# Experts' outputs by accumulating scatters: a two-layer decoder on one core, rows added in memory in place of gathers and sums

## The chip, the cores and the metric

One core of a Trainium2 chip runs the whole program. The metric is the device time of one execution in microseconds (us), the median of several runs. Engines are named as the profile names them: PE (TensorE), DVE (VectorE), ACT (ScalarE), POOL (GpSimd), SP (SyncE, which here only issues transfers).

## The reference, cut to what matters

`x` holds 4 batches of 512 tokens of 512 floats. Six sublayers follow one another, each added to its input:

```python
x = x + attn0(layernorm(x))              # linear attention and softmax attention
x = x + graph(ctx_512, layernorm(x))     # graph mixing
x = x + moe(layernorm(x))                # the experts
x = x + attn1(layernorm(x))              # self attention
x = x + xattn1(layernorm(x), ctx_512)    # causal cross attention
x = x + ffn1(layernorm(x))               # gated network with a Walsh-Hadamard transform
```

The part that the change touches is `moe`, cut to its core (T = 2048 tokens):

```python
scores = softmax(x @ w_cls.T)                       # 64 choices: 32 experts, 32 that give nothing
_, topk_idx = top_k(scores + bias, 8)
w = scores[topk_idx]; w = w / (w.sum(-1) + EPS) * 1.5
routed = topk_idx < 32
w_r, w_z = where(routed, w, 0), where(routed, 0, w)
# up to CAP = 256 tokens of each expert, in the order of their numbers
y = (silu(g) * u) @ w_down                          # g, u = split(rows @ w_gate_up)
out = sum over the 8 choices of w_r * y[expert, place] * (1 + w_z.sum())
```

## The kernel before, in words

The program is a chain of stages with a barrier between them, each a function: linear attention (names with `a_`), `graph_and_router` (`gr_`, L1543), `experts` (`ex_`, L2396), `attention_layers` (`at_`, L195), `network` (`ff_`). All matrices are float32; a product is made of three matmuls of high and low parts (`_hi`, `_lo`), and the parts are split off by ACT (high) and DVE or POOL (low).

**Router.** `graph_and_router` treats a batch of 512 tokens (4 tiles of 128) at a time. In `router` (L2171 to L2272) DVE takes the 64 biased scores of each token, finds the 8 largest and their numbers (`max`, L2198, and `max_index`, L2202), makes one-hot rows `hot` of 32 choices x 64 (L2206), sums them to `mask` (L2209), multiplies `hot` with the scores (L2220) and reduces (L2221) to the 8 weights; PE counts each expert's earlier tokens (`choices`), and from the places DVE makes two things: the table `index`, which says for each of the 32 x 256 slots which token fills it (`write_rows`, L2274), and `slots`, which says for each of a token's 8 choices in which slot its output will lie (`slot_numbers`, L2252 to L2261). `weights` keeps the 8 weights of a token. In between, DVE searches the 153rd largest value of half of the graph's rows (`max` and `match_replace`, L2050, L2056), and ACT and POOL that of the other half by bisection; the two meet at L2101. On POOL, `blocks_hot` (L2345 to L2355) waits for DVE's row numbers, and `rstds` (L2341) for its statistics. The layer normed rows go to `normed` in memory, one row of 512 floats for each token behind a row 0 of zeros, and x to `x_after_graph`.

**Experts.** 32 experts in turn, two buffers (`u`). POOL gathers the expert's 256 rows of `normed` by two indirect transfers (L2645, four experts ahead), PE transposes them (L2505) and makes the products, POOL splits off the low part of `w_down` (`split_d`, L2635, two experts ahead), SP loads 1.5 MB of weights for each (L2455). The output y is copied from PSUM by ACT (tile 0, L2577) and DVE (tile 1, L2610), and SP stores its 512 KB to `out_rows` (L2461). Between two experts DVE makes two steps of the Walsh-Hadamard transform of another layer's weights (`butterfly`, L2622). The engines' programs are straight queues: an instruction that waits holds all behind it on its engine.

**Attention.** For each batch, each token's 8 output rows are gathered from `out_rows` by `slots` (POOL, `gather`, L262 to L272: 32 transfers of 128 rows a batch) and added into x with their weights (DVE, `add_rows`, L274 to L291, 32 times `scalar_tensor_tensor`), and x goes back to memory by `store_sum` (L293) as the residual that `load_residual` reads later. Batch 0 is done in a block of its own, `first_sums` (L297 to L313), before anything else of the attention; batches 1 to 3 are spread over the steps of the attention by `SUMS_AT` and `sums_at` (L355 to L361). A step `g` is one of 4 groups of heads of a batch, three steps ahead of the softmax for the projections. Layer norm is `measure`, `statistics`, `layernorm` (L731 to L750).

```python
SUMS_AT = {1: 0, 6: 1, "mid_end": 2, "end": 3}     # L355: after which pair of a step the adds stand
first_sums: load x of batch 0; 32 gathers; 32 adds, 4 bn_stats; 4 stores of 256 KB
```

## Time and profile before

| | before |
|---|---|
| median of 3 runs | 3035.86 us (3032.19 to 3039.69) |
| span of the profiled execution | 3028.2 us, 7.7 us under that median |
| mean granted clock of TensorE | 0.900 |
| PE busy | 2476.7 us (82%) |
| DVE busy | 1884.0 us (62%) |
| ACT busy | 1239.5 us (41%) |
| POOL busy | 851.9 us (28%) |
| written to memory | 62.92 MB |
| read from memory | 182.30 MB |

The span of the profiled execution runs from its first to its last instruction; its own time as a run is not listed apart from the three. The stages lie at 0 to 655 us (linear attention), 655 to 1140 (graph and router), 1140 to 1482 (experts), 1482 to 1536 (`first_sums`), 1536 to 2493 (the two attentions) and 2493 to 3028 (network). A share of busy time is a mean over stages that have different limits, so each stage has to be read by itself.

### The profile page before, as it was taken

How to read it: one execution, taken by the hardware profiler on the slowest of the kernel's cores; microseconds unless marked ns; L12 is line 12 of the kernel's file. 1: busy time of each engine (PE TensorE's matmuls, PEld its weight loads, DVE VectorE, ACT ScalarE, POOL GpSimd, SP SyncE). 2: the span in 40 equal slices, each digit the busy share in tenths (PEclk: the TensorE clock that was granted, in tenths of full speed). 3: DMA queues.
4: the chain of work that ended last, by engine and by line, in shares of the span. 5: the costliest groups of instructions: out<-in, count | busy, mean ns of one | idle time of the engine just before them, and what ended most of it. 6: DMA issues, size and time to landing. Idle time of an engine off the chain costs nothing. (4 is left out here: it accounts for less than half of the span.)

```text
span 3028.2 us, 35090 instructions
## 1 busy us (share of the span) xinstructions
PE 2476.7 (82%) x12822; PEld 1644.7 (54%) x12822; DVE 1884.0 (62%) x2959; ACT 1239.5 (41%) x1873; POOL 851.9 (28%) x1176
## 2 busy tenths in 40 slices
PE   5898989864443357999448999999999879999999
PEld 4454545321222237998334554545555538888887
DVE  3766575627899985778557777565655444444443
ACT  2444444428656625666103433334333323333332
POOL 2232222215657634555343332001211110000000
PEclk8999999976665678999768999999999979999999
DMA  3213132212222346988585655334433423101000
GB/s 117 65 43 84 43 84 46 70 61 77 77 80 77 108 163 213 308 300 289 158 185 136 159 146 157 88 89 104 109 95 91 115 80 127 42 0 42 1 28 15
DMA packets 186940, 323.55 MB, mean 107 GB/s; under 512 B 20450, under 2 KB 52066, under 8 KB 186788
## 3 DMA queue, kind: packets, MB, share of 16 engines
q1 hardware_dynamic: 168356, 270.44, 30.0%
q0 software_dynamic: 15360, 50.34, 6.3%
q8 instruction: 88, 1.44, 0.2%
q10 hardware_dynamic: 3072, 0.79, 0.1%
q14 instruction: 64, 0.52, 0.1%
HBM read 182.30 MB, written 62.92 MB: 81 GB/s over the span
## 5 line engine op out<-in xcount | busy, mean ns | idle before, releaser
L757 DVE TENSOR_REDUCE at_negmax<-at_ps 128x2 f32<-128x1024 f32 (+3 forms) x256 | 259.1, 1016 | 120.3 <-PE at_ps L523 63.1
L670 ACT ACTIVATE at_probs<-at_ps 128x1024 f32<-128x1024 f32 (+3 forms) x256 | 221.7, 866 | 267.4 <-PE at_ps L538 263.3
L1367 DVE TENSOR_REDUCE a_negmax<-a_ps 128x2 f32<-128x1024 f32 x128 | 155.2, 1217 | 136.4 <-PE a_ps L1120 135.8
L59 PE MATMUL ff_ps<-ff_xnT_hi,ff_s_hi 128*128 128x512 f32 x512 | 200.8, 392 | 5.1 <-DVE ff_xnT_lo L2878 5.1
L60 PE MATMUL ff_ps<-ff_xnT_lo,ff_s_hi 128*128 128x512 f32 x512 | 200.1, 391 | 0.0
L61 PE MATMUL ff_ps<-ff_xnT_hi,ff_s_lo 128*128 128x512 f32 x512 | 200.1, 391 | 0.0
L1946 ACT ACTIVATE gr_act_signs<-gr_signed,gr_test 128x512 bf16<-128x512 f32 x248 | 177.4, 717 | 42.3 <-POOL gr_test L2339 20.4
L2908 DVE TENSOR_TENSOR ff_hid<-ff_hid,ff_ps 128x512 f32<-128x512 f32 x64 | 44.0, 688 | 238.6 <-ACT ff_hid L2853 238.6
L538 PE MATMUL at_ps<-at_qk 98*128 98x512 f32 (+3 forms) x512 | 171.7, 417 | 21.0 <-DMA at_qk<-at_mrow 10.6
L1268 ACT ACTIVATE a_probs<-a_ps 128x1024 f32<-128x1024 f32 x128 | 130.8, 1023 | 135.2 <-PE a_ps L1138 134.6
L518 PE MATMUL at_ps<-at_qk 96*128 96x512 f32 (+3 forms) x512 | 162.9, 382 | 19.0 <-DVE at_xnT_lo L818 8.9
L538 PEld LDWEIGHTS at_ps<-at_qk 98*128 98x128 f32 x512 | 83.3, 194 | 162.5 <-issue 93.6
L2853 ACT ACTIVATE ff_hid<-ff_ps 128x512 f32<-128x512 f32 x64 | 38.3, 598 | 303.3 <-PE ff_ps L61 303.3
L59 PE MATMUL ex_ps<-ex_x_hi,ex_gu_hi 128*128 128x256 f32 x512 | 148.4, 290 | 6.3 <-issue 5.8
L60 PE MATMUL ex_ps<-ex_x_lo,ex_gu_hi 128*128 128x256 f32 x512 | 145.7, 285 | 0.0
L61 PE MATMUL ex_ps<-ex_x_hi,ex_gu_lo 128*128 128x256 f32 x512 | 145.6, 284 | 0.0
L852 POOL TENSOR_SCALAR_AFFINE_SELECT at_probs<-at_probs 128x256 f32<-128x256 f32 x128 | 52.4, 411 | 291.4 <-ACT at_probs L670 291.4
L782 DVE RECIPROCAL at_weighed<-at_weighed 128x128 f32<-128x128 f32 x128 | 119.7, 939 | 15.2 <-ACT at_weighed L705 15.2
L2635 POOL TENSOR_TENSOR ex_d_lo<-first_d,ex_d_hi 128x1024 fp32r<-128x1024 f32 x32 | 87.4, 2730 | 136.5 <-ACT ex_d_hi L2561 136.4
L873 POOL TENSOR_TENSOR at_oT<-at_weighed 128x512 f32<-128x512 f32 x32 | 40.7, 1270 | 296.6 <-DVE at_weighed L782 296.6
L726 ACT CAST at_part<-at_ps 128x512 fp32r<-128x512 f32 x64 | 37.4, 587 | 211.7 <-PE at_ps L61 200.7
L630 PE MATMUL at_ps<-at_wo,at_oT 128*128 128x512 f32 x256 | 115.9, 607 | 6.8 <-POOL at_oT L873 6.6
(431 smaller groups left out, 6640.1 us busy)
## 6 DMA issues: line engine op xcount, KB each, us to landing
at_qk<-at_part SPq DMA_DIRECT2D x384, 128.0 KB
first_gu<-in_L_ffn_w_gate_up_dram SPq DMA_DIRECT2D x32, 1024.0 KB, 13.4
a_qk<-a_part SPq DMA_DIRECT2D x192, 128.0 KB
first_d<-in_L_ffn_w_down_dram SPq DMA_DIRECT2D x32, 512.0 KB, 13.6
out_rows<-ex_y SPq DMA_DIRECT2D x32, 512.0 KB
gr_aside_raw<-in_L_ffn_W_dram SPq DMA_DIRECT2D x48, 256.0 KB, 3.1
w13T<-gr_aside_out SPq DMA_DIRECT2D x32, 256.0 KB, 3.2
shared_x<-x_after_cross SPq DMA_DIRECT2D x8, 1024.0 KB
```

Of the source, the lines that this page charges most:

```text
L59: pe.matmul(out, lh, rh, start=start, stop=False, skip_group_check=True)
L60: pe.matmul(out, lh, rl, start=False, stop=False, skip_group_check=True)
L61: return pe.matmul(out, ll, rh, start=False, stop=stop, skip_group_check=True)
L518: mm = pe.matmul(bank(key, i, 0, n), qk[0:KROWS, g % STACKS, 0, j, t * P:(t + 1) * P], qk[0:KROWS, g % STACKS, 1, j, 0:n], start=True, sto ...
L538: mm = pe.matmul(bank(key, i, lo), qk[0:KROWS + 2, g % STACKS, 1, j, t * P:(t + 1) * P], qk[0:KROWS + 2, g % STACKS, 0, j, lo:S], start=Tr ...
L630: mm = pe.matmul(bank(key, i), oT[:, dc, t * P:(t + 1) * P], woT[:, dc, :], start=dc == 0, stop=dc == NC - 1, skip_group_check=True)
L670: act.activation(probs[:, t % 2, 2 * w:2 * w + 2, lo:S], banks(("kq", g, s), lo), ACT.Exp, scale=SCALE).then_inc(free(("kq", g, s)), 1)
L757: dve.reduce_max(negmax[:, g % 2, :].rearrange("p (j t) -> p j t", t=NT)[:, 2 * w:2 * w + 2, t], banks(("qk", g, s), 0, width(g, t)), AX.X ...
L782: dve.reciprocal(weighed[:, 1, t * P:(t + 1) * P], weighed[:, 1, t * P:(t + 1) * P]).then_inc(rec_done, 1)
L1268: act.activation(probs[:, t % 2, 2 * w:2 * w + 2, :], banks(("kq", g, s)), ACT.Exp, scale=SCALE).then_inc(free(("kq", g, s)), 1)
L1367: dve.reduce_max(negmax[:, g % 2, :].rearrange("p (j t) -> p j t", t=NT)[:, 2 * w:2 * w + 2, t], banks(("qk", g, s)), AX.X, negate=True).t ...
L1946: act.activation(act_signs[:, j, :], src, ACT.Sign, scale=-1.0, bias=against, accum_out=total[:, i, j:j + 1]).then_inc(counted_to[j], 1)
```

## The change

- **Router.** A token's row in `normed` becomes 544 floats: 512 of x and 32 gates, one for each expert (0 where the expert is not among the 8). The mask is had by striking out the 8 largest (`match_replace`) and comparing; the gates are scores x mask, normalised, one 128x128 tensor for a batch, which SP stores (`store_gates`). Numbers of slots, one-hot rows, `slots` and `weights` are gone. `MASK` and `ROUTE_STEPS` are the counts of DVE's steps that a semaphore goes by.
- **Experts.** The gathers fetch 544 floats, DVE keeps the expert's gate column (`keep_gate`), ACT and DVE scale y by it as they copy it. POOL scatters y: two indirect transfers of 128 rows, which add each row into the token's row of `x_rows` in memory. Empty slots go to 256 spare rows of `x_rows`, so that no row comes twice in one expert. The scatter of one expert waits until that of the expert before has landed, since both may hold the same token. SP's stores of y are gone. ACT's loop is written out, where it was a hardware loop over pairs of experts.
- **Attention.** `first_sums`, all gathers, adds and stores of sums are gone; x is read from `x_rows`. The four `bn_stats` of a batch stand in `measure`, as for the cross attention before.

```diff
-            if j % UNITS_T == UNITS_T - 1:
-                dve.wait_ge(added, GROUP * (n + 1))
-                dve.memset(add_carrier[:, n // UNITS_T:n // UNITS_T + 1], 0.0)
-                dve.bn_stats(stats[:, t, :], xs(b)[:, t, :]).then_inc(stat, 1)
...
-            sp.wait_ge(added, GROUP * (UNITS_B * b + UNITS_T * (t + 1)))
-            sp.dma_start(sum_rows[b, t], xs(b)[:, t, :]).then_inc(sum_out, 16)
...
-                for j in range(UNITS_B):
-                    gather(pool, 0, j)
...
-                for j in range(UNITS_B):
-                    add_rows(dve, 0, j)
...
-        SUMS_AT = {1: 0, 6: 1, "mid_end": 2, "end": 3}
-
-        def sums_at(g, when):
...
-                sp.dma_start(res[:], mid_pairs[b - B, u] if cross(b) else sum_pairs[b, u]).then_inc(res_in, 16)
+                sp.dma_start(res[:], mid_pairs[b - B, u] if cross(b) else in_pairs[b, u]).then_inc(res_in, 16)
...
-                for n, j in sums_at(g, "end"):
-                    store_sum(sp, n, j // UNITS_T)
...
+            for t in range(NT):
+                measure(0, t)
             statistics(0)
             layernorm(0)
...
-                    for b, j in sums_at(g, s):
-                        add_rows(dve, b, j)
-                    if g % NC == 0 and 2 <= s < 2 + NT and B <= g // NC + 1 < ALL:
+                    if g % NC == 0 and 2 <= s < 2 + NT and 1 <= g // NC + 1 < ALL:
...
-                        for b, j in sums_at(g, ("mid_end", "end")[i]):
-                            add_rows(dve, b, j)
...
                 sp.dma_start(normed_tiles[b], xn[:, b % 2]).then_inc(normed_out, 16)
+
+            def store_gates(b):
+                sp.wait_ge(gates_done, b + 1)
+                sp.dma_start(gate_tiles[b], gates[:, b % 2]).then_inc(gates_out[b % 2], 16)
...
-                    mx = dve.max_index(top_i[:, t, :], top_v[:, t, :], biased[:, t, :])
+                    mx = dve.match_replace(struck_out[:, t, :], top_v[:, t, :], biased[:, t, :], 2 * NEG)
                 step(mx)
-                step(dve.tensor_copy(choice[:], top_i[:].rearrange("p t k -> p (t k)")))
-
-                step(dve.tensor_tensor(hot[:].rearrange("p t k e -> p (t k) e"), bcast_mid(iota[:], NT * TOPK),
-                                       bcast_last(choice[:], NT * TOPK, E_ALL), ALU.is_equal))
-                with nc.allow_low_precision(reason="zeros and ones"):
-                    step(dve.tensor_reduce(mask[:], hot[:, :, :, 0:E_ROUTED].rearrange("p t k e -> p t e k"), AX.X, ALU.add), wait=False)
+                step(dve.tensor_tensor(mask[:], biased[:], struck_out[:], ALU.not_equal))
...
-                step(dve.tensor_scalar(k8[:, 1, :], choice[:], float(E_ROUTED), None, ALU.is_lt))
...
                 def gate_weights():
-                    for u in range(2):
-                        for i in range(2):
-                            t = 2 * u + i
-                            step(dve.tensor_tensor(prod[:, i], hot[:, t], bcast_mid(score[:, t, :], TOPK), ALU.mult), wait=i == 1)
-                        step(dve.reduce_sum(k8[:, 0, 2 * u * TOPK:2 * (u + 1) * TOPK], prod[:].rearrange("p t k e -> p (t k) e"), AX.X))
-                    step(dve.reduce_sum(r4[:, 3, :], per_token(0), AX.X))
+                    if b >= 2:
+                        dve.wait_ge(gates_out[b % 2], 16 * (b // 2))
+                    step(dve.tensor_tensor(picked[:], score[:], mask[:], ALU.mult))
+                    step(dve.reduce_sum(r4[:, 3, :], picked[:], AX.X))
+                    step(dve.reduce_sum(r4[:, 5, :], picked[:, :, E_ROUTED:E_ALL], AX.X))
...
-                    step(dve.tensor_tensor(per_token(0), per_token(0), bcast_last(r4[:, 4, :], NT, TOPK), ALU.mult))
-
-                    step(dve.tensor_tensor(k8[:, 2, :], k8[:, 0, :], k8[:, 1, :], ALU.mult))
-                    step(dve.tensor_tensor(k8[:, 0, :], k8[:, 0, :], k8[:, 2, :], ALU.subtract))
-                    step(dve.reduce_sum(r4[:, 5, :], per_token(0), AX.X))
-                    step(dve.tensor_scalar(r4[:, 5, :], r4[:, 5, :], 1.0, None, ALU.add))
-                    step(dve.tensor_tensor(per_token(2), per_token(2), bcast_last(r4[:, 5, :], NT, TOPK), ALU.mult))
+                    step(dve.tensor_tensor(r4[:, 5, :], r4[:, 5, :], r4[:, 4, :], ALU.mult))
+                    step(dve.scalar_tensor_tensor(out=r4[:, 5, :], in0=r4[:, 5, :], scalar=1.0, in1=r4[:, 4, :], op0=ALU.add, op1=ALU.mult))
+                    dve.tensor_tensor(gates[:, b % 2], picked[:, :, 0:E_ROUTED], bcast_last(r4[:, 5, :], NT, E_ROUTED), ALU.mult).then_inc(gates_done, 1)
...
-                    dve.scalar_tensor_tensor(out=row[:], in0=row[:], scalar=1.0, in1=chosen, op0=ALU.add, op1=ALU.mult).then_inc(decoding, 1)
-
-                def slot_numbers():
-                    for t in range(NT):
-                        step(dve.tensor_tensor(picked_places[:, t], hot[:, t, :, 0:E_ROUTED], bcast_mid(place[:, t, :], TOPK), ALU.mult),
-                             wait=t == NT - 1)
-                    step(dve.reduce_sum(k8[:, 3, :], picked_places.rearrange("p t k e -> p (t k) e"), AX.X))
-
-                    step(dve.tensor_scalar(k8[:, 5, :], k8[:, 3, :], float(CAP), None, ALU.is_lt))
-                    step(dve.tensor_tensor(k8[:, 5, :], k8[:, 5, :], k8[:, 1, :], ALU.mult))
-                    step(dve.scalar_tensor_tensor(out=k8[:, 4, :], in0=choice[:], scalar=float(CAP), in1=k8[:, 3, :], op0=ALU.mult, op1=ALU.add))
-                    step(dve.scalar_tensor_tensor(out=k8[:, 4, :], in0=k8[:, 4, :], scalar=-float(SLOTS), in1=k8[:, 5, :], op0=ALU.add, op1=ALU.mult))
-                    step(dve.tensor_scalar(k8[:, 4, :], k8[:, 4, :], float(SLOTS), None, ALU.add))
-                    dve.tensor_copy(slots[:, at:at + NT * TOPK], k8[:, 4, :]).then_inc(slots_done, 1)
...
-            def store(i, u):
-                y_act[u].wait(sp, i, 1)
-                y_dve[u].wait(sp, i, 1)
-                sp.dma_start(y_dram[bass.ds(i * 2 + u, 1)].rearrange("e p t d -> (e p) t d"), y[:, u]).then_inc(y_out[u].sem, 16)
...
-                y_out[u].wait(act, i, 0)
-                act.copy(y[:, u, 0, :], ps[:, 6, :]).then_inc(y_act[u].sem, 1)
+                if i:
+                    y_out[u].wait(act, i - 1, 16 * CT)
+                gate_kept[u].wait(act, i, 1)
+                act.activation(y[:, u, 0, :], ps[:, 6, :], ACT.Copy, scale=gate[:, (2 * i + u) % 4, 0:1]).then_inc(y_act[u].sem, 1)
...
+            def keep_gate(i, u):
+                e = 2 * i + u
+                rows_in[u].wait(dve, i, 16 * CT)
+                if e >= 4:
+                    y_act[u].wait(dve, i - 2, 1)
+                    y_dve[u].wait(dve, i - 2, 1)
+                dve.tensor_copy(gate[:, e % 4, :], rows[:, u, :, D + e]).then_inc(gate_kept[u].sem, 1)
+
             def split_x(i, u):
+                keep_gate(i, u)
...
-                y_out[u].wait(dve, i, 0)
-                dve.tensor_copy(y[:, u, 1, :], ps[:, 7, :]).then_inc(y_dve[u].sem, 1)
+                if i:
+                    y_out[u].wait(dve, i - 1, 16 * CT)
+                gate_kept[u].wait(dve, i, 1)
+                dve.tensor_scalar(y[:, u, 1, :], ps[:, 7, :], gate[:, (2 * i + u) % 4, 1:2], None, ALU.mult).then_inc(y_dve[u].sem, 1)
...
+            dve.tensor_scalar(empty[:], index[:], 0.5, None, ALU.is_lt).then_inc(emptied, 1)
+            dve.wait_ge(emptied, 1)
+            dve.wait_ge(spare_made, 1)
+            by_tile = empty[:].rearrange("p (e t) -> p e t", t=CT)
+            dve.tensor_tensor(by_tile, by_tile, spare_rows[:].rearrange("p (o t) -> p o t", o=1).to_broadcast([P, E_ROUTED, CT]), ALU.mult).then_inc(emptied, 1)
+            dve.wait_ge(emptied, 2)
+            dve.tensor_tensor(index_out[:], index[:], empty[:], ALU.add).then_inc(out_index, 1)
...
+            def scatter(e):
+                i, u = e // 2, e % 2
+                y_act[u].wait(pool, i, 1)
+                y_dve[u].wait(pool, i, 1)
+                if e == 0:
+                    pool.wait_ge(out_index, 1)
+                else:
+                    y_out[(e - 1) % 2].wait(pool, (e - 1) // 2, 16 * CT)
+                for t in range(CT):
+                    at = column(e, t)
+                    pool.indirect_dma_start(x_rows, bass.IndirectOffsetOnAxis(index_out[:, at:at + 1], 0), y[:, u, t, :], None,
+                                            compute_op=ALU.add).then_inc(y_out[u].sem, 16)
...
             def gather(e):
                 i, u = e // 2, e % 2
                 turned[u].wait(pool, i, 0)
+                gate_kept[u].wait(pool, i, 0)
                 for t in range(CT):
...
                     split_d(e // 2 + 1, e % 2)
+                scatter(e)
+            for u in range(2):
+                y_out[u].wait(pool, PAIRS - 1, 16 * CT)
```

DVE in the router, the steps behind the 8 largest values, batch 0. Before (`gr_prod` are one-hot rows times scores, `gr_k` the 8 values of a token):

```order
L2202 MAX_INDEX gr_top_i<-gr_top_v,gr_logit 128x8 x4
L2204 CAST gr_choice<-gr_top_i 128x32
L2206 TENSOR_TENSOR gr_hot<-gr_iota,gr_choice 128x2048
L2209 TENSOR_REDUCE gr_mask<-gr_hot 128x128
L2214 TENSOR_SCALAR gr_k<-gr_choice 128x32
L2220 TENSOR_TENSOR gr_prod<-gr_hot,gr_expd 128x512 x2
L2221 TENSOR_REDUCE gr_k<-gr_prod 128x16
L2220 TENSOR_TENSOR gr_prod<-gr_hot,gr_expd 128x512 x2
L2221 TENSOR_REDUCE gr_k<-gr_prod 128x16
```

and now (`gr_struck_out` are the scores without the 8 largest, `gr_picked` those of the mask):

```order
L2098 MATCH_REPLACE gr_struck_out<-gr_top_v,gr_logit 128x64 x4
L2100 TENSOR_TENSOR gr_mask<-gr_logit,gr_struck_out 128x256
L2106 TENSOR_TENSOR gr_picked<-gr_expd,gr_mask 128x256
L2107 TENSOR_REDUCE gr_r<-gr_picked 128x4
L2108 TENSOR_REDUCE gr_r<-gr_picked 128x4
L2109 TENSOR_SCALAR gr_r<-gr_r 128x4
L2110 RECIPROCAL gr_r<-gr_r 128x4
L2111 TENSOR_SCALAR gr_r<-gr_r 128x4
L2112 TENSOR_TENSOR gr_r<-gr_r 128x4
L2113 SCALAR_TENSOR_TENSOR gr_r<-gr_r 128x4
L2114 TENSOR_TENSOR gr_gates<-gr_picked,gr_r 128x128
```

The instructions of 128x2048, 128x1024 and 128x512 are gone, the largest left has 256 columns; the eleven rows are the whole of the mask and the weights.

POOL at the start of the experts. Before (`ex_rows` are the gathered rows, `ex_d_lo` the low part of `w_down`):

```order
L2645 DMA ex_rows<-normed,index 128x512 x4
L2635 TENSOR_TENSOR ex_d_lo<-first_d,ex_d_hi 128x1024 x2
L2645 DMA ex_rows<-normed,index 128x512 x6
L2635 TENSOR_TENSOR ex_d_lo<-first_d,ex_d_hi 128x1024
L2645 DMA ex_rows<-normed,index 128x512 x2
L2635 TENSOR_TENSOR ex_d_lo<-first_d,ex_d_hi 128x1024
```

and now:

```order
L2534 IOTA ex_spare_rows 128x2
L2532 DMA ex_rows<-normed,index 128x544 x4
L2505 TENSOR_TENSOR ex_d_lo<-first_d,ex_d_hi 128x1024 x2
L2532 DMA ex_rows<-normed,index 128x544 x6
L2505 TENSOR_TENSOR ex_d_lo<-first_d,ex_d_hi 128x1024
L2523 DMA x_rows<-ex_y,ex_index_out 2305x512 x2
L2532 DMA ex_rows<-normed,index 128x544 x2
L2505 TENSOR_TENSOR ex_d_lo<-first_d,ex_d_hi 128x1024
```

A scatter (`x_rows<-ex_y`) stands behind the gathers for the expert four ahead and the `split_d` for the one two ahead, and ahead of those for the next expert.

DVE at the start of the attention. Before (L286 is an add of a gathered row, here of batch 1):

```order
L749 TENSOR_SCALAR shared_x<-shared_x,at_mv,at_rstd 128x512 x4
L786 MEMSET at_ones 128x32
L286 SCALAR_TENSOR_TENSOR shared_x<-shared_rows,weights,shared_x 128x512 x4
L818 TENSOR_TENSOR at_xnT_lo<-at_ps,at_xnT_hi 128x1024 x2
L286 SCALAR_TENSOR_TENSOR shared_x<-shared_rows,weights,shared_x 128x512 x2
L829 TENSOR_TENSOR at_part<-at_ps,at_part 128x512
L286 SCALAR_TENSOR_TENSOR shared_x<-shared_rows,weights,shared_x 128x512 x2
L290 MEMSET at_add_carrier 128x1
L291 BN_STATS at_stats<-shared_x 128x6
L829 TENSOR_TENSOR at_part<-at_ps,at_part 128x512
```

and now:

```order
L649 TENSOR_SCALAR shared_x<-shared_x,at_mv,at_rstd 128x512 x4
L688 MEMSET at_ones 128x32
L718 TENSOR_TENSOR at_xnT_lo<-at_ps,at_xnT_hi 128x1024 x2
L727 TENSOR_TENSOR at_part<-at_ps,at_part 128x512 x2
L730 MEMSET at_qk 2x2048
L727 TENSOR_TENSOR at_part<-at_ps,at_part 128x512 x2
```

The adds are gone from between the low parts of the transposed x (`at_xnT_lo`) and of the projections (`at_part`).

## Rows read from the trace of the kernel before

**Rows 1.** Windows of the trace: busy us of each engine, granted clock, DMA share, GB/s

```profile
core 0: us, PE busy (x) PEld busy (x) DVE busy (x) ACT busy (x) POOL busy (x), PEclk, DMA share, GB/s
1200.00:1300.00 100.00, 100.00 (x724) 94.08 (x723) 74.12 (x64) 65.42 (x69) 53.08 (x32) 1.00 0.89 306
1475.00:1535.00 60.00, 0.00 (x0) 0.00 (x0) 27.74 (x42) 0.00 (x0) 34.16 (x33) 0.52 0.76 197
```

**Rows 2.** Timeline of DVE, y of the first, the 15th and the last expert

```profile
1174.57 0.69 DVE L2610 COPY ex_y<-ex_ps 128x512 f32<-128x512 f32 x1 [4.45 <-PE ex_ps L61]
1305.85 0.69 DVE L2610 COPY ex_y<-ex_ps 128x512 f32<-128x512 f32 x1
1474.47 0.69 DVE L2610 COPY ex_y<-ex_ps 128x512 f32<-128x512 f32 x1 [5.58 <-PE ex_ps L61]
```

**Rows 3.** Groups of DVE by line, 650 to 1145 us: busy us, mean ns

```profile
L2206 DVE TENSOR_TENSOR gr_hot<-gr_iota,gr_choice 128x2048 bf16<-128x2048 f32 x4 | 9.2, 2292 | 0.1
L2209 DVE TENSOR_REDUCE gr_mask<-gr_hot 128x128 bf16<-128x1024 bf16 x4 | 7.5, 1880 | 0.1
L2220 DVE TENSOR_TENSOR gr_prod<-gr_hot,gr_expd 128x512 f32<-128x512 bf16 x16 | 10.4, 694 | 0.2
L2221 DVE TENSOR_REDUCE gr_k<-gr_prod 128x16 f32<-128x1024 f32 x8 | 9.8, 1220 | 0.3
L2252 DVE TENSOR_TENSOR gr_prod<-gr_hot,gr_place 128x256 f32<-128x256 bf16 x16 | 5.9, 429 | 0.0
```

**Rows 4.** Timelines of POOL and DVE around the second batch of the router

```profile
857.32 2.85 POOL L2355 TENSOR_SCALAR gr_block_hot<-gr_block_hot,gr_token 128x1024 bf16<-128x1024 bf16 x1
862.03 1.04 POOL L2343 TENSOR_TENSOR gr_rstd<-gr_mv,minus_half 128x4 f32<-128x4 f32 x1 [1.86 <-DVE gr_mv L2075]
861.86 0.74 DVE L2101 TENSOR_SCALAR_CACHE_REDUCE gr_dve_flags<-gr_signed,gr_test 128x512 bf16<-128x512 f32 x1
868.48 0.23 DVE L2084 TENSOR_SCALAR gr_blend<-gr_rstd,gr_gam 128x4 f32<-128x4 f32 x1
```

**Rows 5.** Timelines of POOL and DVE, the ends of first_sums

```profile
1482.96 0.19 POOL L268 TENSOR_TENSOR at_pool_carrier<-minus_half 128x1 f32<-128x1 f32 x1 [24.45 <-ACTq L298]
1534.69 0.69 DVE L291 BATCH_NORM_STATS2 at_stats<-shared_x 128x6 f32<-128x512 f32 x1
1535.73 0.18 DVE L739 BATCH_NORM_AGGREGATE at_mv<-at_stats 128x2 f32<-128x6 f32 x1 [0.35 <-PEq L298]
```

**Rows 6.** Transfers of the whole span: KB each, us from issue to landing

```profile
first_d<-x_after_attn SPq DMA_DIRECT2D x4, 1024.0 KB, 5.6
```

**Rows 7.** Timelines of ACT and DVE at the start of the attention

```profile
1542.69 1.01 ACT L716 CAST at_xnT_hi<-at_ps 128x1024 fp32r<-128x1024 f32 x1 [0.69 <-PE at_ps L594]
1544.00 1.54 DVE L286 SCALAR_TENSOR_TENSOR shared_x<-shared_rows,weights,shared_x 128x512 f32<-128x512 f32 x2 [4.40 <-issue]
1548.84 2.35 DVE L818 TENSOR_TENSOR at_xnT_lo<-at_ps,at_xnT_hi 128x1024 fp32r<-128x1024 f32 x2
1576.28 1.07 ACT L726 CAST at_part<-at_ps 128x512 fp32r<-128x512 f32 x2 [10.19 <-DMA at_qk<-at_part]
1612.74 1.02 ACT L670 ACTIVATE at_probs<-at_ps 128x1024 f32<-128x1024 f32 x1 [3.00 <-PE at_ps L538]
```

**Rows 8.** Timeline of POOL, oT at the same point of three batches

```profile
1777.25 1.27 POOL L873 TENSOR_TENSOR at_oT<-at_weighed 128x512 f32<-128x512 f32 x1 [18.58 <-DVE at_weighed L782]
1899.39 1.27 POOL L873 TENSOR_TENSOR at_oT<-at_weighed 128x512 f32<-128x512 f32 x1 [24.70 <-DVE at_weighed L782]
2023.23 1.27 POOL L873 TENSOR_TENSOR at_oT<-at_weighed 128x512 f32<-128x512 f32 x1 [24.72 <-DVE at_weighed L782]
```

**Rows 9.** Timeline of POOL in the experts: a split_d and a gather

```profile
1236.61 0.95 POOL L2645 DMA_INDIRECT ex_rows<-normed,index  x1 [0.30 <-issue]
1241.36 2.94 POOL L2635 TENSOR_TENSOR ex_d_lo<-first_d,ex_d_hi 128x1024 fp32r<-128x1024 f32 x1 [3.80 <-ACT ex_d_hi L2561]
```

**Rows 10.** Line 270, its transfers

```profile
DMA to landing us min/median/max: 3.9/4.9/7.4
```

184 lines of the change are left out of this document (47 added, 137 removed).

## The prediction, made before the changed kernel was run

> **What bounds the kernel now.** I read the windows by stage first, since the stages have different limits. In the experts PE is busy 100.00 of 100 us, at its full clock, while the DMA engines are busy 0.89 of the time and move 306 GB/s [rows 1]: PE is the bound, and the transfers stand close behind it. From the first y to the last on DVE there are 31 periods in 299.9 us, 9.67 us each; the first 14 take 9.38 each, the last 17 9.92 [rows 2]. In the stage behind them PE does nothing: in 60 us DVE works 27.74 and POOL 34.16 [rows 1], all of it gathers and adds of batch 0. In the router DVE is the engine that the others wait for: POOL's last work of a batch ends at 860.17 and its next instruction waits 1.86 us for DVE [rows 4]. In the attention proper the softmax on PE and the exponentials set the pace, and DVE's adds may or may not lie beside them. So the change has four places, and I cost each by itself, against the profiled span of 3028.2 us. The median of the runs is 7.7 above it, and I add the same 7.7 in the end.
>
> **Router.** Per batch DVE loses the 128x2048 comparison 2.29, the mask's reduction 1.88, four products 2.78, two reductions 2.44, four products of 256 columns 1.72 [rows 3] and, with their reduction and some 20 operations of 128x32, 16.3 us. It gains a comparison and a product of 128x256 at the 0.43 of such a row [rows 3], two reductions and eight small ones: 3.4 us. Net 12.9 a batch. Not all of it shows, because DVE and POOL meet twice in a batch. DVE came 1.86 later than POOL at the statistics, and from the end of rstd (863.07) to DVE's use of it (868.48) another 5.4 lies in hand [rows 4]; past these 7.3 us DVE waits for POOL's table and bisection instead. Three batches are followed by a next one: 3 x 7.3 = 21.9. In the last batch the path through the mask to the rows is shorter by 2.29 + 1.88 - 0.43 = 3.7, and the rest of the weights lies beside the index work. Sum **-26**; bounds: -9 if only POOL's wait is to be had (3 x 1.86 + 3.7), -42 if all 12.9 show (3 x 12.9 + 3.7). The stores of the gates (4 of 64 KB, on SP's queue behind the normed rows) are needed only at the end of the stage, and I cost them at nothing; cover gone, one landing more.
>
> **First sums.** From 1482.96 to 1535.73 the block takes 52.8 us [rows 5]. In its place stand the load of x, 5.6 us for the same megabyte [rows 6], and four bn_stats of 0.69 [rows 5]: 8.4. The end of the experts gets longer: before, a plain store was awaited, now one scatter has to land before the last one is issued; I add 3. Sum **-41**; bounds -44 and -36.
>
> **Start of the attention.** DVE's order changes there as the third piece of the order above shows. The high part of x's transposed tiles is done at 1543.70 [rows 7], but two adds of 1.54 and the wait for their rows hold DVE, and the low parts run from 1548.84 to 1551.19. Without the adds the first low part goes in ACT's 1.7 us between its two halves and the second ends at 1544.9: -6.3. The stacks of q and k are awaited 10.19 us before 1576.28 [rows 7], with the gathers in the same DMA engines (7.2 to 7.4 to land there, 3.9 with little beside them [rows 10]): I take -4, between 0 and -8. Adds between the low parts of the projections, between the maxima and ahead of the memset, four pairs of 1.54 with a bn_stats of 0.69, of which PE waits for some 7.2. Sum **-17.5** until the first exponential at 1612.74 [rows 7]; bounds -8 and -26.
>
> **The rest of the attention.** oT at the same point of three batches: 122.1 us between the first two, with adds and gathers in them, 123.8 between the last two, without [rows 8]. So the 96 adds lie under other work, and I take **0**, down to -6.
>
> **Experts.** Nothing of the scatter is in this trace, so I bound it. Below: SP's stores are gone and ACT's loop is written out, so the 9.38 of the first 14 periods could hold throughout: 31 x (9.38 - 9.67) = -9. Two things can stretch it. First bytes: 306 GB/s at a share of 0.89 is 344 GB/s for full engines [rows 1], 2.87 MB in a period of 9.38. If an addition in memory reads the old row too, 0.52 MB come on top, and 0.03 for the gates: 3.42 MB, 9.95 us. Second the chain: POOL may issue scatter e only when scatter e-1 has landed, so a period is at least the first issue (0.95 + 0.30 [rows 9]) and the landing of the second. Landings of POOL's gathers are 3.9 at least, 4.9 in the middle, 7.4 at most [rows 10]; the DMA engines are fuller here, so I take the upper one, and 1.5 for the second reading (0.52 MB at 344): 1.25 + 7.4 + 1.5 = 10.15. Both come to 10 to 10.2; I take 10.2: 31 x 0.53 = **+16**. From above: a landing of twice 7.4, 1.25 + 14.8 = 16.05 us, +198. POOL itself has room: split_d 2.94 [rows 9], four issues of 1.25, 8.0 of 10.2 us; its wait for the scatter holds the next gathers (four experts ahead) and the next split_d (two ahead), so a scatter late by less than a period holds nobody else. The scaling of y replaces a copy of the same shape, and keep_gate is a few columns: 32 x 0.1, inside DVE's idle time.
>
> The Trainium skill, Collectives: The Full Stack, section "The bandwidth ceiling: the fold count and why AG ≠ RS ≠ AR", says that an adding transfer is slow not for its arithmetic but because it reads two sources on one ring, and gives 32.35 against 62.28 GB/s. By it y's transfers cost double, which is the reading in the sum above; by the row of before alone, y costs what its plain store did, and this term would be 0 and the time 2951. The Trainium skill, DMA: Bandwidth & Descriptors, section on the anatomy of one DMA, says that the completion, above all of a write to memory, is the dominant fixed cost. That rule speaks against this change, where each expert's scatter waits for a completion; no row here shows a landing of a write by POOL.
>
> **Sum.** -26 - 41 - 17.5 + 0 + 16 = -68.5: span 2959.7, median 3035.9 - 68.5 = **2967.4**.
>
> **The rivals.**
> - *The experts do not get slower.* PE stays the bound at 9.38, since a write that no one awaits soon costs only share. For it: 0.11 of the DMA engines are free. Against: the bytes worked out to 9.95. -26 - 41 - 17.5 - 9 gives 2942.
> - *Scatters land late, but the change still gains.* Reading and writing each queue behind the weights: 1.25 + 7.4 + 2 x 1.5 = 11.65 a period, +61: 3012.
> - *The chain of landings decides* (slower than before). Each scatter waits for the one before; gains elsewhere are 84.5, so the point is a period of 9.67 + 84.5 / 31 = 12.4 us, a landing over 11.1. At the upper bound of 14.8, 2967.4 - 16 + 198 = 3149. For it: the wait is unconditional, and nothing of the kind was measured. Against: POOL's gathers, which share the engines with as much, never took over 7.4 [rows 10]. PE would then idle in each period, and its granted clock could fall below the 1.00 of [rows 1], on top.
> - *The router gains nothing.* POOL's and ACT's bisection turns out to be the bound as soon as DVE is shorter. The 1.86 us of waiting speak against. 2967.4 + 26 = 2993.
>
> **Chances.** A measurement of this kernel tells 0.3% from nothing, about 9 us. My forecast (2950 to 2985) 0.42; no loss in the experts 0.20; late scatters 0.18, of which 0.02 within 9 us of before; the router without gain 0.09; the chain decides 0.11, of which 0.01 within 9 us. Faster by over 0.3%: 0.42 + 0.20 + 0.16 + 0.09 = 0.87; within 0.3%: 0.03; slower: 0.10. The range has to hold the forecast, the first two rivals and the last, so it goes from 2935 (2942, with some of the attention's -6) to 3020 (3012 and a little more); what it leaves out is the chain, 0.11, and the far ends.
>
> **What would show it.** In the profile of the changed kernel: DVE's y of the experts every 10.2 us, with a wait of POOL ahead of each scatter and a DMA share near 1 (step right), or 9.4 (first rival), or over 12.4 with PE idle (chain). PE's pause between the experts and the attention far shorter than the 60 us of [rows 1]. In the router the row L2355 followed without a wait for DVE. The three distances of oT unchanged near 122 to 124. Wrong would be above all a scatter whose landing grows with the load of the other queues, and a router whose four batches keep their distances.

## The result, and the profile after

| | before | changed |
|---|---|---|
| median | 3035.38 us (4 runs, 3032.19 to 3039.69) | 2963.23 us (4 runs, 2959.4 to 2973.69) |
| ratio | | 0.9766, 95% interval 0.9744 to 0.9788 |
| profiled execution | span 3028.2 us | 2973.69 us, span 2971.9 us |

The gain is 72.2 us of the median, where 68.5 was forecast, and 2963.2 lies in the range of 2935 to 3020 that was given. The profiled execution of the changed kernel is the longest of its four, so the stages of its trace add up to less gain than the medians show. From its page, the span, the busy time of each engine, and what went to and from memory:

```profile
span 2971.9 us, 34593 instructions
PE 2490.0 (84%) x12822; PEld 1649.0 (55%) x12822; DVE 1772.6 (60%) x2762; ACT 1224.7 (41%) x1859; POOL 800.9 (27%) x1064
HBM read 149.79 MB, written 58.98 MB: 70 GB/s over the span
```

The bytes written fell from 62.92 to 58.98 MB, those read from 182.30 to 149.79. To see where the time went I take the same five instructions in both traces: DVE's first memset of the router, y of the first and of the last expert, the arrival of x in the attention, its first aggregate:

```profile
679.60 0.09 DVE L1923 MEMSET gr_taken<- 128x32 f32 x1 [3.27 <-PEq L44]
1149.33 0.75 DVE L2473 TENSOR_SCALAR ex_y<-ex_ps,ex_gate 128x512 f32<-128x512 f32 x1 [4.34 <-PE ex_ps L52]
1480.19 0.75 DVE L2473 TENSOR_SCALAR ex_y<-ex_ps,ex_gate 128x512 f32<-128x512 f32 x1 [4.70 <-PE ex_ps L52]
1500.07 2.47 DVE L635 BATCH_NORM_STATS2 at_stats<-shared_x 128x6 f32<-128x512 f32 x4 [17.99 <-DMA shared_x<-x_rows]
1502.58 0.18 DVE L641 BATCH_NORM_AGGREGATE at_mv<-at_stats 128x2 f32<-128x6 f32 x1
```

and on ACT a wait for the stacks of q and k, and the first exponential:

```profile
1531.07 1.07 ACT L628 CAST at_part<-at_ps 128x512 fp32r<-128x512 f32 x2 [4.15 <-DMA at_qk<-at_part]
...
1562.50 1.02 ACT L572 ACTIVATE at_probs<-at_ps 128x1024 f32<-128x1024 f32 x1 [2.73 <-PE at_ps L440]
```

The distances between them, beside those of before from [rows 2], [rows 5] and [rows 7] (the router's first memset was at 669.88 there), in us:

| stage | before | changed | difference | forecast |
|---|---|---|---|---|
| up to the router's first memset | 669.9 | 679.6 | +9.7 | 0 |
| router, to the first y | 504.7 | 469.7 | -35.0 | -26 |
| experts, first y to last y | 299.9 | 330.9 | +31.0 | +16 |
| last y to the first aggregate | 61.3 | 22.4 | -38.9 | -41 |
| to the first exponential | 77.0 | 59.9 | -17.1 | -17.5 |
| to the end | 1415.5 | 1409.4 | -6.1 | 0 |
| span | 3028.2 | 2971.9 | -56.3 | -68.5 |

The first line is the linear attention, which the change does not touch. In the twelve later runs, none of which touches it either, it ended at 668.4 to 677.5 us (after_again's at 671.5); so most of the 9.7 us is chance, and without them the profile agrees better with the medians: -66. The first sums and the start of the attention are right within some 2 us, the router and the experts were off by 9 and by 15 in opposite directions. The experiments are about those two.

The rows that answer to [rows 8], oT at the same point of three batches on POOL:

```profile
1719.52 1.28 POOL L766 TENSOR_TENSOR at_oT<-at_weighed 128x512 f32<-128x512 f32 x1 [24.75 <-DVE at_weighed L682]
...
1840.99 1.28 POOL L766 TENSOR_TENSOR at_oT<-at_weighed 128x512 f32<-128x512 f32 x1 [24.75 <-DVE at_weighed L682]
...
1964.96 1.28 POOL L766 TENSOR_TENSOR at_oT<-at_weighed 128x512 f32<-128x512 f32 x1 [24.75 <-DVE at_weighed L682]
```

121.5 and 124.0 us, where before had 122.1 and 123.8: the adds had been hidden. The gain of the rest came earlier, in the first batch: 157.0 us from the first exponential to the first of these rows, 164.5 before [rows 7, 8]. Its 6.1 us in all lie at the bound that the forecast had given.

### The profile page after: what moved, and what is told of

It is laid out like the page before. It is cut to its first block and busy times, and to the rows that moved or that the text cites. A ratio compares the mean times of both kernels' runs of the same rounds, so it can differ in the third digit from the quotient of the medians.

```text
span 2971.9 us, 34593 instructions
## 1 busy us (share of the span) xinstructions
PE 2490.0 (84%) x12822; PEld 1649.0 (55%) x12822; DVE 1772.6 (60%) x2762; ACT 1224.7 (41%) x1859; POOL 800.9 (27%) x1064
## 3 DMA queue, kind: packets, MB, share of 16 engines
HBM read 149.79 MB, written 58.98 MB: 70 GB/s over the span
## 5 line engine op out<-in xcount | busy, mean ns | idle before, releaser
L440 PE MATMUL at_ps<-at_qk 98*128 98x512 f32 (+3 forms) x512 | 171.8, 418 | 17.6 <-DMA at_qk<-at_mrow 10.9
L2523 POOL DMA_INDIRECT x_rows<-ex_y,ex_index_out x64 | 130.1, 2033 | 55.9 <-DMA x_rows<-ex_y,ex_index_out 43.0
L727 DVE TENSOR_TENSOR at_part<-at_ps,at_part 128x512 fp32r<-128x512 f32 x64 | 43.4, 692 | 142.1 <-ACT at_part L628 142.1
```

The lines of the kernel that those rows point to most:

```text
L440: mm = pe.matmul(bank(key, i, lo), qk[0:KROWS + 2, g % STACKS, 1, j, t * P:(t + 1) * P], qk[0:KROWS + 2, g % STACKS, 0, j, lo:S], start=Tr ...
L2523: pool.indirect_dma_start(x_rows, bass.IndirectOffsetOnAxis(index_out[:, at:at + 1], 0), y[:, u, t, :], None, compute_op=ALU.add).then_inc ...
```

## Experiments

Five of the runs were executed once: less_bytes (2954.88 us), sp_store_gate_on_act (2922.65), pad12 (2975.29), pad30 (2979.18) and pad_ahead (2988.49). Of them only a stage is read, since single times of one kernel lie up to 20 us apart. The others have four or five executions, and their median is given.

**The changed kernel again**, no edit, as the measure for the stages of the others.

> The changed kernel once more, for the spread of its stages. Its first profiled execution had the linear attention, which the change does not touch, end 9.7 us later than before; if that is chance, this one has it within 3 us of before, and the experts (first y to last y on DVE) again near 331 us, 31 above before. Ratio 0.973 to 0.979.

2965.20 us, ratio 0.9782 (0.9764 to 0.9801). Router 470.2, experts 330.9 again, last y to aggregate 22.6. That the experts are the same to 0.1 us in these two executions is more than can be counted on: in pad12, pad30 and pad_ahead below, whose edits lie in the router alone, they took 326.8, 324.7 and 331.6 us. So up to 7 us between two traces of this stage say nothing.

### What the scatters cost

In the window that answers to [rows 1], the columns as there:

```profile
core 0: us, PE busy (x) PEld busy (x) DVE busy (x) ACT busy (x) POOL busy (x), PEclk, DMA share, GB/s
1200.00:1300.00 100.00, 90.50 (x609) 84.02 (x609) 76.97 (x65) 50.98 (x56) 80.02 (x46) 0.93 0.99 274
```

PE, busy all the time before, has 9.5 us of gaps in 100, its granted clock is 0.93, and the DMA share is 0.99 at fewer GB/s than before. The scatters' line, its issues on POOL (least, median and most in ns) and their landing:

```profile
L2523 POOL DMA_INDIRECT x_rows<-ex_y,ex_index_out x64: 1541/1618/3653, 1153.6 to 1483.8; - x64
DMA to landing us min/median/max: 4.7/7.7/10.6
```

An issue takes 1.6 us in the middle, where [rows 9] has 0.95 for a gather, and lands after 7.7 us, 4.7 to 10.6. Some issues take up to 3.65 us, so the mean is higher: 2.14 us from 1170 to 1420 us, the middle of the experts. On POOL one turn looks so:

```profile
1204.23 2.40 POOL L2505 TENSOR_TENSOR ex_d_lo<-first_d,ex_d_hi 128x1024 fp32r<-128x1024 f32 x1
1209.37 1.61 POOL L2523 DMA_INDIRECT x_rows<-ex_y,ex_index_out  x1 [2.73 <-DMA x_rows<-ex_y,ex_index_out]
```

The scatter waited 2.73 us for the one before, and the gathers for the next expert stand behind it. PE's transposition then waits for rows:

```profile
1211.17 1.11 PE L2354 MATMUL ex_ps<-ident,ex_rows 128*128 128x128 f32 x4 [3.44 <-DMA ex_rows<-normed,index]
```

Three things could be behind the 31 us: bytes, the wait for the landing, and POOL's time.

**plain_scatter.** The scatters write, the sum is left out:

```diff
-  pool.indirect_dma_start(x_rows, ..., y[:, u, t, :], None, compute_op=ALU.add)
+  pool.indirect_dma_start(x_rows, ..., y[:, u, t, :], None)
```

> The scatters write and do not add (the sum of experts' outputs is left out); the wait for the scatter before stays. Bytes theory (reading the old rows fills the DMA engines, share 0.99): the experts lose most of the 31 us, 300 to 310 us from first y to last, share near 0.9. Chain theory (each scatter waits for the landing of the one before): the landing gets shorter by the second reading only, 1 to 2 us of 7.7, and the experts take 305 to 320. Queue theory (an issue of a scatter takes POOL 2.0 us where a gather takes 0.95): the issues stay at 1.6 to 2.0 us and the experts at 325 to 331.

2942.75 us, ratio 0.9717 (0.9702 to 0.9731); experts 304.2 us. Issues and landings:

```profile
L2523 POOL DMA_INDIRECT x_rows<-ex_y,ex_index_out x64: 960/1230/3068, 1141.3 to 1444.2; - x64
DMA to landing us min/median/max: 2.7/7.6/9.5
```

The wait is in the program as before, and the landings are hardly shorter in the middle (7.6 against 7.7), yet 26.7 of the 31.0 us are gone. The edit also shortens POOL's issues (0.96 us at the least for 1.54), so these 26.7 are the price of the addition in all, not that of its bytes alone. (The trace is of the fastest of the five executions; by the medians the run is 22.5 us under after_again.) The share of the DMA engines in the middle of the experts (1170 to 1420 us), q0 is POOL's queue; first the changed kernel:

```profile
q1 hardware_dynamic: 28598, 41.18, 51.6%
q0 software_dynamic: 10304, 24.88, 45.1%
```

then plain_scatter:

```profile
q0 software_dynamic: 7935, 26.80, 32.1%
```

and of the kernel before, where q0 holds only gathers:

```profile
q0 software_dynamic: 4006, 13.12, 14.5%
```

A gather costs 14.5% of 250 us for 13.12 MB, 2.76 us of all 16 engines a MB, so 1.54 us for an expert's 0.557 MB. The changed kernel's q0 takes 45.1% of a period of 10.67, 4.81 us: 3.27 are left for the scatter's 0.524 MB. In plain_scatter it is 32.1% of 9.81, 3.15 us: 1.61. So the addition about doubles the engines' time for a scatter (2.03 times). This is an estimate: the same sum gives 3.09 us in own_rows, 3.20 in no_split_d and 3.89 in less_bytes, 1.9 to 2.4 times the 1.61. The Trainium skill, Collectives: The Full Stack, section "The bandwidth ceiling: the fold count and why AG ≠ RS ≠ AR", has a factor of two between a ring's ReduceScatter and its AllGather, and gives two source reads as the reason. This trace agrees in time, with 3.27 against 1.61. The reading of the old row itself does not show in the counted bytes: the pages of both runs have 149.79 MB read and 58.98 MB written. All queues of the changed kernel together take 96.7% of 10.67 us, 10.3 us an expert: that is the bound the forecast put at 9.95.

**own_rows.** The additions go to rows of each expert's own, so that none waits for the one before (the sum into x is left out):

```diff
-  y_out[(e - 1) % 2].wait(pool, (e - 1) // 2, 16 * CT)
-  pool.indirect_dma_start(x_rows, ...(index_out[:, at:at + 1], 0), y[:, u, t, :], ...)
+  pool.indirect_dma_start(own_rows, ...(slot_of[:, at:at + 1], 0), y[:, u, t, :], ...)
```

> Each expert's outputs are added into rows of its own (memory of 8192 rows that nobody reads; the sum into x is left out), so that no scatter waits for the one before; additions, issues and bytes as in the changed kernel. Chain theory: the experts fall to 300 to 310 us. Bytes theory: they stay at 325 to 331 with a DMA share of 0.99. Queue theory: 320 to 331, POOL's gathers later than before by the longer issues.

2958.40 us, ratio 0.9763 (0.9749 to 0.9776); experts 325.4 us. Issues and landings:

```profile
L2523 POOL DMA_INDIRECT own_rows<-ex_y,ex_slot_of x64: 1542/1879/3590, 1144.3 to 1469.0; - x64
DMA to landing us min/median/max: 5.0/8.6/10.0
```

The experts are 5.5 us shorter, less than the 7 us that traces of unchanged experts differ by; the median is 6.8 us under that of after_again, with intervals that just overlap (0.9749 to 0.9776, 0.9764 to 0.9801). So the wait for the landing by itself is worth 5 to 7 us of the 31, if it is worth anything; with it gone the additions land later (8.6 us in the middle).

**less_bytes.** Half of `w_gate_up` is not loaded:

```diff
-  sp.dma_start(raw_gu[:, u], gu_dram[e])
+  sp.dma_start(raw_gu[:, u, 0:NC // 2], gu_dram[e, :, 0:NC // 2])
```

> Only half of w_gate_up is loaded for each expert (0.5 MB of 3.4 MB less; the other half keeps the first experts' values, so the products are not those of the reference), scatters as in the changed kernel. Bytes theory: the experts fall from 331 us to 300 to 312, DMA share under 0.9, scatter landings under 7. Queue theory (POOL's issue of an adding scatter, 1.54 us where a plain one takes 0.96, and DVE's and POOL's holding each other up): they stay at 322 to 331.

Experts 320.7 us, 10.2 less than the changed kernel and between the two forecasts. In the same window as above:

```profile
1200.00:1300.00 100.00, 90.59 (x646) 83.66 (x646) 83.58 (x68) 52.61 (x59) 86.00 (x47) 0.98 0.90 227
```

The share is 0.90, landings 6.6 us in the middle. The engines are no longer full, and 21 of the 31 us are still there. So bytes alone are not the cause of all of it. The waits from 1170 to 1420 us (total, times, longest) tell what is left. The changed kernel has

```profile
ACT ex_gu_hi L2406 <- DMA first_d<-in_L_ffn_w_down_dram: 31.9, 14, 4.6
PE ex_ps L2354 <- DMA ex_rows<-normed,index: 18.6, 12, 3.4
```

and less_bytes

```profile
PE ex_ps L2354 <- DMA ex_rows<-normed,index: 21.1, 12, 4.3
ACT ex_gu_hi L2406 <- DMA first_d<-in_L_ffn_w_down_dram: 0.4, 1, 0.4
```

ACT no longer waits for weights, but PE waits for the gathered rows as before, and these are issued by POOL behind the scatters. POOL has nearly no time left there: of the 250 us it is busy 213.3, and 24.3 more are the 0.30 us between two issues. In plain_scatter it is 213.9 and 26.6. On DVE the low part of `w_gate_up` takes 3.62 us in the mean (2.60 in the changed kernel, 2.29 alone), which may have taken a part of the bytes' place as well; this run does not tell.

**no_split_d.** POOL leaves out its 2.41 us of `split_d` from the third expert on:

```diff
-  pool.tensor_tensor(flat(d_lo[:, u]), flat(raw_d[:, u]), flat(d_hi[:, u]), ALU.subtract)
+  pool.sem_inc(d_lo_done[u].sem, 1)        # experts 2 to 31
```

> The changed kernel without POOL's split_d (2.41 us an expert) from the third expert on; the low part of w_down stays that of the first two experts, so the products are not those of the reference. All transfers, bytes, issues and waits of the scatters stay. Queue theory (POOL's time, with 1.54 us for the issue of an adding scatter, and its holding DVE up, make what the bytes do not): the experts fall from 331 us to 300 to 312. Bytes and chain theory (DMA share 0.95 to 0.99 and the wait for landings): they stay at 322 to 331, with POOL's wait for the landing longer by what split_d covered.

2965.30 us, ratio 0.9787 (0.9758 to 0.9815); experts 331.2 us, unchanged. Its waits (total, times, longest):

```profile
POOL x_rows L2526 <- DMA x_rows<-ex_y,ex_index_out: 83.5, 21, 6.5
```

What `split_d` had covered turned into waiting for the landing: 83.5 us in 21 times between 1180 and 1420, where the changed kernel waits 23.0. As the only cause, POOL's time falls: the period of the changed kernel does not need it, since the transfers (share 0.96 from 1170 to 1420) and their landings (7.5 us in the middle) make it by themselves. But POOL's time is close behind: busy and between issues it has 226.8 of the 250 us in the changed kernel, and it is what less_bytes and plain_scatter run into once the transfers are lighter. That is read from the traces; no run took both away.

### Why the experts were not at 300 even without scatters

**sp_store.** No scatter; SP stores y plainly, as before (the sum is left out):

```diff
-  scatter(e)                                             # POOL
+  sp.dma_start(y_dram[...], y[:, u]).then_inc(y_out[u].sem, 32)   # SP, between the loads
```

> No scatters: SP stores y plainly, as in the kernel before (the sum of experts' outputs is left out); gates, scaling and the wider gathers as changed. All theories: experts at 291 to 300 us, which gives the whole price of the scatters; if it is above 303, the scaling, keep_gate or the wider rows cost something that I put at nothing.

2943.69 us, ratio 0.9714 (0.9701 to 0.9727); experts 317.3 us, outside of what I had written (291 to 300), and slower than the plain scatters. On DVE a butterfly and the next low part:

```profile
1237.94 3.77 DVE L2498 TENSOR_TENSOR shared_x<-shared_x 128x1024 f32<-128x1024 f32 x1
1245.72 2.29 DVE L2455 TENSOR_TENSOR ex_gu_lo<-first_gu,ex_gu_hi 128x2048 fp32r<-128x2048 f32 x1 [0.59 <-ACT ex_gu_hi L2419]
```

and on POOL in the same turn:

```profile
1238.20 2.42 POOL L2518 TENSOR_TENSOR ex_d_lo<-first_d,ex_d_hi 128x1024 fp32r<-128x1024 f32 x1
1244.52 0.96 POOL L2545 DMA_INDIRECT ex_rows<-normed,index  x1 [3.90 <-DVE ex_gate L2467]
1245.79 3.04 POOL L2545 DMA_INDIRECT ex_rows<-normed,index  x1 [0.30 <-issue]
```

The butterfly, 1.21 us in the changed kernel, takes 3.77 beside `split_d`, and the second gather's issue, 0.96 like the first's when nothing is in its way, takes 3.04 beside DVE's low part. It is so in nearly every turn: in the mean 3.3 us for the butterfly and 1.90 for an issue. The gathers now wait for `keep_gate` on DVE (3.90 us of idle time), which places them there.

**sp_store_gate_on_act.** The same, with the gate column copied by ACT:

```diff
-  dve.tensor_copy(gate[:, e % 4, :], rows[:, u, :, D + e])
+  act.copy(gate[:, e % 4, :], rows[:, u, :, D + e])
```

> As sp_store (plain stores by SP, sum left out), with keep_gate on ACT in place of DVE. sp_store took 317.3 us in the experts, with the butterfly at 3.3 us and every second gather's issue at 3.0, because the gathers waited for keep_gate and so fell beside DVE's operations of two inputs. If that alignment is the cause: 300 us or less, butterfly under 2.2 us. If the wider rows or the scaling cost the 17 us: 314 to 318 again.

Experts 300.2 us: 17.1 us less for a copy of two columns on another engine, and as good as the 299.9 of before. The groups of the butterfly and of the gathers (busy, mean ns | idle before):

```profile
L2498 DVE TENSOR_TENSOR shared_x<-shared_x 128x1024 f32<-128x1024 f32 x20 | 50.8, 2539 | 0.0
L2545 POOL DMA_INDIRECT ex_rows<-normed,index x47 | 46.9, 998 | 59.2 <-ACT ex_gate L2431 50.8 <-issue 8.2
```

The butterfly went from 3.3 to 2.54 us (I had expected under 2.2), the gathers' issue from 1.90 to 1.00. The wider rows and the scaling cost nothing that shows. What moved with the copy is the place of the gathers beside DVE's work, and with it the collisions; that they are the 17 us fits all these rows, and the run has no other difference.

**gate_act_one_load** has that edit in the changed kernel, and the attention's second load of x only when the first has landed:

```diff
+            sp.wait_ge(xs_in[0], 16)
             load(sp, 1)
```

> The changed kernel with keep_gate on ACT, and with the attention's second load of x issued only when the first has landed. Alignment theory (DVE's copy of the gates waits 1.2 us for POOL, and the gathers wait for it): the experts fall from 331 to 310 to 322 us; if the scatters' own bytes and issues are all of it, 327 to 331. The load: both megabytes left at once and x came 5 us after its issue, with DVE at 22.5 us behind the last y; alone it should land 1 to 3 us sooner, 20 to 21.5. Ratio to before 0.969 to 0.976.

2963.71 us, ratio 0.9779 (0.9757 to 0.9800), the same as the changed kernel's 0.9782. Experts 328.7: with scatters the copy's place is worth nothing that can be told (2.2 us, inside the spread). Last y to the first aggregate 24.2, not sooner: the single load is no gain.

**gate_act_ahead_one_load** sets each scatter one turn later as well, between the gathers and `split_d`:

```diff
+                if e: scatter(e - 1)
                 if e + 2 < E_ROUTED: split_d(...)
-                scatter(e)
```

> As that one, and each scatter one turn later in POOL's program, between the gathers and split_d, so that a gather is not behind a scatter that waits for its landing. Chain theory (worth 5.5 us by own_rows): experts 2 to 6 us under the run beside it. Rival: y's two buffers come free later and ACT and DVE wait for them ahead of y, same or up to 10 slower.

2974.77 us, ratio 0.9814 (0.9790 to 0.9837); experts 337.7, 9 slower: ACT now waits 69.0 us between 1180 and 1420 for y's buffers. The rival was right. No version that computes the whole beats the changed kernel.

### What the router gave

**pad12 and pad30** put 12 and 30 reductions of 128x256 behind the mask, in the first three batches:

```diff
+                for k in range(30 if b < B - 1 else 0):
+                    dve.reduce_sum(pad[:, b, k, :], struck_out[:], AX.X)
```

> 12 reductions of 128x256 (0.42 us each, 5.0 in all) on DVE behind the mask, in the first three batches. By the step of my prediction, only 7.3 of the 12.9 us that DVE lost in a batch can show, so 5.0 of padding are free: the router (first memset to first y) stays at 470 us, within 2. Rival, DVE bounds the router all the way (35 of the 42 us came back): 3 x 5.0 = +15, 483 to 486.

> 30 such reductions, 12.6 us a batch, which gives DVE back the load it had. By the step of my prediction 3 x (12.6 - 5.6) = +21, 491; by the rival 3 x 12.6 = +38, 505 to 508, past the 504.7 of before.

Router 477.4 and 487.3 us, for 470.2: neither theory in pad12, and in pad30 near the 491 of the step.

**pad_ahead** puts ten of them ahead of the mask, in all four batches.

> Ten reductions of 128x256 (4.2 us) on DVE ahead of the mask, in all four batches, where before had 4.2 us of one-hot rows and their sum. Behind the mask, 5.0 us of padding cost 2.4 a batch and 12.6 cost 5.7. If the 35 us of the router are those 17 and what stood ahead of the mask in full: 4 x 4.2 = +17, router at 486 to 488 us. If the place does not matter: 4 x 0.45 x 4.2 = +8, 478.

Router 486.9 us, +16.7 over 470.2, as expected.

The whole stage is too coarse a measure for these, since without any padding it lies between 465.8 and 470.2 us in the later runs. The spread is all in its first stretch, up to the mask of the first batch (140.2 to 143.9 us). From mask to mask the distances are the same within 0.1 us in all runs that leave the router as it is. The masks of the four batches on DVE, before:

```profile
812.99 1.89 DVE L2209 TENSOR_REDUCE gr_mask<-gr_hot 128x128 bf16<-128x1024 bf16 x1
918.02 1.88 DVE L2209 TENSOR_REDUCE gr_mask<-gr_hot 128x128 bf16<-128x1024 bf16 x1
1019.20 1.88 DVE L2209 TENSOR_REDUCE gr_mask<-gr_hot 128x128 bf16<-128x1024 bf16 x1
1104.46 1.86 DVE L2209 TENSOR_REDUCE gr_mask<-gr_hot 128x128 bf16<-128x1024 bf16 x1
```

and changed:

```profile
822.71 0.42 DVE L2100 TENSOR_TENSOR gr_mask<-gr_logit,gr_struck_out 128x256 bf16<-128x256 f32 x1
915.88 0.42 DVE L2100 TENSOR_TENSOR gr_mask<-gr_logit,gr_struck_out 128x256 bf16<-128x256 f32 x1
1006.51 0.42 DVE L2100 TENSOR_TENSOR gr_mask<-gr_logit,gr_struck_out 128x256 bf16<-128x256 f32 x1
1082.06 0.43 DVE L2100 TENSOR_TENSOR gr_mask<-gr_logit,gr_struck_out 128x256 bf16<-128x256 f32 x1
```

The distances, with those of the padded traces read in the same way, in us:

| | 1st to 2nd mask | 2nd to 3rd | 3rd to 4th | 4th mask to first y |
|---|---|---|---|---|
| before | 105.0 | 101.2 | 85.3 | 70.1 |
| changed | 93.2 | 90.6 | 75.5 | 67.3 |
| pad12 (5.0 behind the mask) | 97.9 | 93.7 | 78.8 | 66.2 |
| pad30 (12.6 behind) | 101.7 | 98.0 | 81.6 | 66.0 |
| pad_ahead (4.2 ahead) | 98.3 | 94.6 | 78.2 | 68.5 |

So of 5.0 us behind the mask 3.7 show in the mean of three distances, of 12.6 only 7.3, and of 4.2 ahead of it 3.9. What stands ahead of the mask (2.29 of one-hot rows, 1.88 of their sum) has next to no cover, since PE's counts and the table of rows wait for it; what stands behind it is covered for a quarter to two fifths. An estimate from these for the change itself, 3.7 us less ahead and 9.2 less behind, is 3.4 + 5.7 = 9.1 a batch. The change gained 10.7 a batch, so some 1.6 stay unexplained.

## Why the prediction was right, and where it was not

- **Router, forecast -26, measured -35.** The step that failed is "past these 7.3 us DVE waits for POOL's table": from mask to mask 11.9, 10.5 and 9.7 us show, 32.1 in place of 21.9. The last batch gave 2.8 for 3.7. The changed trace, at the batch of [rows 4]; POOL:

```profile
866.06 2.89 POOL L2223 TENSOR_SCALAR gr_block_hot<-gr_block_hot,gr_token 128x1024 bf16<-128x1024 bf16 x1
868.92 1.13 POOL L2211 TENSOR_TENSOR gr_rstd<-gr_mv,minus_half 128x4 f32<-128x4 f32 x1
```

and DVE:

```profile
861.08 0.74 DVE L1997 TENSOR_SCALAR_CACHE_REDUCE gr_dve_flags<-gr_signed,gr_test 128x512 bf16<-128x512 f32 x1
863.39 2.85 DVE L2015 TENSOR_SCALAR first_gu<-first_gu,gr_bound,gr_gam 128x512 f32<-128x512 f32 x2
870.28 0.22 DVE L1980 TENSOR_SCALAR gr_blend<-gr_rstd,gr_gam 128x4 f32<-128x4 f32 x1
```

DVE's statistics were done at 861.17, POOL's table at 868.95, so POOL did become the later one; but rstd was ready at 870.05 and DVE wanted it at 870.28. DVE never waited, since its own operations in between had become longer beside POOL's (two of 0.54 each took 2.85 together, 1.07 before). So DVE stayed the bound at this meeting with POOL, where I had it wait. It is not the bound throughout, or all 12.9 us would show. The measured 35 lay within my bounds of -9 and -42.
- **Experts, forecast +16, measured +31.** The mechanism was right (a period of 10.67 us, forecast 10.2; DMA share 0.97 to 0.99, forecast near 1), the size was not. The addition's second reading was put at 1.5 us and came out at 1.66 (3.27 - 1.61, an estimate as said). A plain scatter runs at 0.524 MB in 1.61 us, 325 GB/s, where I had 344 from a stretch of mostly loads. The landing is 7.7 us, where I had 8.9 with the reading, but POOL's issue is 1.6 us and not 0.95.

  The 7.4 us that I took as the upper landing was from gathers of the attention [rows 10]; beside the weights of the experts gathers now take up to 8.0 and scatters up to 10.6. "POOL itself has room" (8.0 of 10.2) was wrong too: with issues of 2.14 us in the mean POOL has work for 9.9 of 10.9 us an expert. Each bound by itself, 10.3 for the transfers, 9.6 for issue and landing in the middle, 9.9 for POOL, is under the 10.67, so bounds from averages do not make the period.

  The period went from 8.6 to 14.9 us. SP moves an extra megabyte of the transform's weights every fourth expert, at 1197.30, 1240.43, 1284.04, 1326.79, 1371.97 and 1415.69, and the periods of 14.73, 14.93, 12.55 and 12.95 us begin 11 to 13 us behind four of these six (one of 12.79 follows none); the other 27 have 10.2 in the mean, as forecast. Before, with the same transfers and a DMA share of 0.83 from 1170 to 1420 us, no period passed 10.9. This reading, that delays of bounds so close add up in turn and most where a burst falls, fits less_bytes (-10.2) and plain_scatter (-26.7), but no run removed the bursts, or chain and bytes together, so how they share the 31 us stays open.
- **The two rules against the change.** The factor of two of the Trainium skill (Collectives: The Full Stack, as above) holds here for the engines' time, about, and the addition cost 26.7 us, its longer issues included. That completions are the dominant fixed cost, above all of a write to memory (the Trainium skill, DMA: Bandwidth & Descriptors, "Anatomy of one DMA"), no run here shows apart from the rest of a landing: 7.7 us for an adding scatter, 7.6 for a plain one, 5.7 for a gather of nearly the same size, which writes no memory. Without the wait for these landings own_rows was 5.5 us shorter in all, inside the spread. Neither could turn the sign, since the sums that the scatters replace had cost 38.9 + 17.1 = 56 us.
- **First sums, -41 and -38.9.** The load took 5.3 us for 5.6. The end of the experts is longer than I put it: SP's load was issued at 1494.73, 14.5 us behind the last y, where the block before had begun 8.5 behind it. +6 in place of +3.
- **Start of the attention, -17.5 and -17.1.** The wait for the stacks fell from 10.19 us [rows 7] to 4.15, -6 where I had taken -4; the rest together gave a little less.
- **The rest, 0 and -6.1**, at its bound.
- **The rivals.** "The experts do not get slower" and "the chain decides" are both refuted by the period; "scatters land late" (11.65 us) was off by 0.98, where the 10.2 was off by 0.47, to the other side. "The router gains nothing" was wrong by the whole of its term. That the sum came within 4.2 us of the median is in part luck: +15 in one term and -9 in another.

## What to carry to other kernels

An accumulating scatter took the DMA engines about twice the time of a plain one and chains its users by the landing, so it pays where it replaces gathers and sums that stand in the open, not where they lie beside matmuls: the gathers and adds in the open and at the start of the attention gave 56 us, all the later ones at most 6. Before calling an operation free because the engine is idle, look at what it releases: a copy of two columns on DVE set POOL's gathers where they collided with DVE in every turn, 17 us. And cost a removal by its place: 4.2 us ahead of the mask were worth 3.9 a batch, 12.6 behind it only 7.3.
